# A two-attention, two-feed-forward kernel on one core: the second attention's first batch prepared inside the last chunk of the first feed-forward

## The reference, cut to what matters

```python
x = x + ffn0(attention0(x, mask, Wq, Wo), lut, gate_idx, up_idx, down_idx)
x = x + ffn1(attention1(x, cond, W_emb, b_emb, g_norm, W_qkv, g_q, g_k, W_out), Wr, br, Wg, Wu, Wd)
```

```python
xn = rms_norm(x1, g_norm) * (1 + scale) + shift      # one factor per row: rsqrt(mean(x1^2) + eps)
q, k, v = split(xn @ W_qkv)                          # 16 heads of 16
q, k = rms_norm(q, g_q), rms_norm(k, g_k)
o = softmax(q k^T / 4) v ;  result = o + o @ W_out
```

## Time and profile before

| | us |
|---|---|
| median of 3 runs (lowest, highest) | 706.95 (706.39, 708.73) |
| the profiled execution's own time | 707.92 |
| its span | 706.2 |
| PE busy | 580.7 (82%) |
| DVE busy | 419.2 (59%) |
| ACT busy | 326.3 (46%) |
| GpSimd busy | 118.9 (17%) |

### The profile page before, as it was taken

One profiled execution on the slowest core, in us unless ns is written; L12 is line 12 of the kernel. 1 busy time (PEld: TensorE's weight loads), 2 busy tenths in 40 slices (PEclk: granted clock), 3 DMA queues, 4 the chain that ended last, 5 costly groups with the idle time before them and its releaser, 6 DMA issues.

```text
span 706.2 us, 15569 instructions
## 1 busy us (share of the span) xinstructions
PE 580.7 (82%) x5115; PEld 347.5 (49%) x5147; DVE 419.2 (59%) x943; ACT 326.3 (46%) x592; POOL 118.9 (17%) x161
## 2 busy tenths in 40 slices
PE   3798989899976999995688777775199999999992
PEld 1344445455534655552354554443156666666661
DVE  1678698989853334343799999996523333333330
ACT  2456667677752332342677777773022222222220
POOL 4221122121511000000000000000203333322211
PEclk9999899999986999997799999997599999999996
DMA  8844345454851000005556666551101111011110
GB/s 295 202 95 113 90 110 123 113 121 108 156 134 32 1 1 0 0 0 125 159 120 150 149 147 148 132 137 46 24 22 46 45 45 41 31 37 37 45 32 3
DMA packets 29413, 60.27 MB, mean 85 GB/s; under 512 B 5989, under 2 KB 16647, under 8 KB 26952
## 3 DMA queue, kind: packets, MB, share of 16 engines
q1 hardware_dynamic: 20624, 25.68, 12.4%
q0 software_dynamic: 6432, 18.46, 12.2%
q10 hardware_dynamic: 2328, 15.75, 9.6%
HBM read 58.75 MB, written 7.81 MB: 94 GB/s over the span
## 4 chain that ended last, share of the span: by engine, by line
PE 27%; DVE 14%; issue 7%; ACT 3%; DVEq 1%; DMA 0%; POOL 0%; POOLq 0%; ACTq 0%
PE PA L1134 8%; PE PD L1153 7%; PE PB L1134 7%; PE PC L1142 2%; DVE arena L1479 2%; DVE small L1451 1%; ACT small L661 1%; DVE ms L1405 1%; DVE newt L1373 1%; PE PB L1020 1%; DVE rs L1379 1%; DVE newt L1376 1%; DVE small L1433 1%; DVE small L1437 1%; PE PD L1122 1%
## 5 line engine op out<-in xcount | busy, mean ns | idle before, releaser
L1231 DVE TENSOR_REDUCE nmax<-PB 128x2 f32<-128x512 f32 x128 | 85.5, 681 | 27.0 <-PE PB L808 25.4
L529 ACT ACTIVATE probs<-PC 128x512 f32<-128x512 f32 x128 | 73.9, 609 | 21.6 <-PE PC L820 20.6
L737 ACT CAST probs<-PC 128x1024 bf16<-128x1024 f32 x19 | 19.2, 1012 | 113.7 <-PE PC L1142 113.7
L1625 DVE TENSOR_TENSOR probs<-PC,probs 128x1024 bf16<-128x1024 f32 x19 | 23.3, 1225 | 80.9 <-ACT probs L737 80.9
L1134 PE MATMUL PA<-arena,probs 128*128 x227 | 53.7, 387 | 7.6 <-issue 3.8
L808 PE MATMUL PB<-small 64*128 64x256 bf16 x256 | 52.4, 297 | 8.2 <-DVE nmax L1231 6.1
L1153 PE MATMUL PD<-arena,probs 128*128 x456 | 54.5, 277 | 2.5 <-issue 2.5
L820 PE MATMUL PC<-small 64*128 64x256 bf16 x256 | 48.1, 289 | 3.8 <-DVE small L1247 3.5
L1153 PEld LDWEIGHTS PD<-arena,probs 128*128 128x128 bf16 x456 | 45.0, 99 | 9.0 <-issue 3.2
L1134 PE MATMUL PB<-arena,probs 128*128 x210 | 48.6, 379 | 0.9
L444 POOL DMA_DIRECT2D arena<-in_w_all x16 | 8.5, 532 | 236.7 <-DVE arena L1479 139.5
(11 more groups left out here) (201 smaller groups left out, 1163.9 us busy)
## 6 DMA issues: line engine op xcount, KB each, us to landing
arena<-idx_low ACTq DMA_DIRECT2D x15, 1024.0 KB
wst<-in_w_all SPq DMA_DIRECT2D x48, 256.0 KB, 2.7
arena<-in_w_all POOLq DMA_DIRECT2D x16, 384.0 KB, 5.9
arena<-in_idx_all SPq DMA_DIRECT2D x1, 2176.0 KB, 10.1
arena<-in_cond SPq DMA_DIRECT2D x16, 128.0 KB, 9.3
small<-in_x SPq DMA_DIRECT2D x16, 128.0 KB, 10.0
arena<-idx_low POOLq DMA_DIRECT2D x2, 1024.0 KB, 14.9
tok_r<-rows SPq DMA_DIRECT2D x1, 2048.0 KB, 14.4
```

What stands on the lines that cost most here:

```text
L529: nc.scalar.activation(probs[:, c, o], PC[:, o], ACT.Exp, scale=SCALE0).then_inc(S["ex"], 1)
L1231: v.tensor_reduce(nmax[:, c, s, :], PB[:, s * 512:(s + 1) * 512].rearrange("p (a k) -> p a k", k=T), AX.X, ALU.max, negate=True).then_inc( ...
L1625: v.tensor_tensor(hT_lo, PC[:], hT_hi, ALU.subtract).then_inc(S["hTl"], 1)
```

## The change

In the first attention, GpSimd's body(i) waits for `ct` of batch i-2 before it makes the product for batch i+2, and `max_columns` writes the absent column first, ahead of the last maximum. In the feed-forward all four chunks are written out; the down sums stand in PC alone, two to a bank, and DVE adds them with two instructions in place of four. PD is so free, and `turn_x(0)`, `queries_keys(0)`, `values1(0)`, `turn_x(1)` with ACT's and DVE's part of them stand between the pieces of chunk 3. The row factors are computed for batches 0 to 7 in chunk 2, and for batches 8 to 15 behind body1(0).

```diff
             def body(i, par, half, before=True, after=True):      # GpSimd
+                if before:
+                    pool.wait_ge(S["ct"], i - 1)
                 if after:
                     pool.wait_ge(S["pq"], 2 * i + 2)
                     projected(i + 2, par, half)
...
+            def totals(c):                                        # ACT
+                for t in range(TPC):
+                    sum_squares(TPC * c + t)
+            def earlier(c):
+                return lambda m: totals(c - 1) if m == MT // 2 - 1 else None
+            def meanwhile3(m):
+                if m == 0:
+                    act.wait_ge(S["gcol"], 6)
+                    act.wait_ge(S["rstd"], 2 + 3 * NEWTON)
+                    scaled(0)
+                if m == 1:
+                    modulated(0, PD)
+                if m == 2:
+                    squares(0, PD)
+                    scaled(1)
+                if m == 3:
+                    values1(0, 0, PD)
+                    totals(2)
+                if m == 4:
+                    modulated(1, PD)
+            gate_chunk(0, lambda m: None)
+            gate_chunk(1, earlier(1))
+            gate_chunk(2, earlier(2))
+            gate_chunk(3, meanwhile3)
...
             high_parts(0)
             body1(0, 0, before=False)
+            totals(3)
             body1(1, 1, before=False)
+            act.wait_ge(S["rstd"], 2 * (2 + 3 * NEWTON))
...
                     for t in range(TPC):                          # PE, down(m)
-                        o = (PC, PD)[t // 2][:, (t % 2) * 512:(t % 2) * 512 + T]
+                        o = PC[:, t * T:(t + 1) * T]
...
-                up(0)
-                if isinstance(c, int):
-                    outputs0(LAST)
-                    norm_and_router()
-                for m in range(1, MT):
+                for m in range(MT):
                     up(m)
-                    down(m - 1)
+                    if m > 0:
+                        down(m - 1)
+                    between(m)
                 down(MT - 1)
-            chunk(0)
-            with pe.Fori(1, TOK // CH) as c:
-                chunk(c)
...
+            def meanwhile3(m):                                    # PE
+                if m == 0:
+                    pe.wait_ge(S["c"], B)
+                    pe.wait_ge(S["w2"], 1)
+                    pe.wait_ge(S["wqkv"], 16)
+                    turn_x(0, PD)
+                if m == 1:
+                    queries_keys(0, PD)
+                if m == 2:
+                    values1(0, PD)
+                if m == 3:
+                    turn_x(1, PD)
...
-            turn_x(0)
-            queries_keys(0)
-            values1(0)
-            turn_x(1)
+            pe.wait_ge(S["hf"], MT * (TOK // CH))
+            pe.wait_ge(S["x1"], B)
             body1(0, 0, before=False)
...
             def max_columns(b):                                   # DVE
-                dve.wait_ge(S["max"], 8 * b + 8)
+                cols = mcol.rearrange("p q r (s m) -> p r s q m", s=2)
                 unless_first(dve, S["mt"], b)
+                v.tensor_copy(mcol[:, :, :, ROW_ABSENT::64].rearrange("p q r s -> p q (r s)"),
+                              nbig[:, :, bass.ds(b, 1)].broadcast_to([P, KT, 2 * PAIRS])).then_inc(S["mc"], 1)
+                maximum(b, 3, 1)
+                dve.wait_ge(S["max"], 8 * b + 8)
                 v.tensor_copy(cols[:, :, :, :, ROW_MAX], nmax[:]).then_inc(S["mc"], 1)
...
-                for t in range(TPC):                              # DVE, end of a chunk
+                for t in range(0, TPC, 2):
+                    o = slice(TPC * c + t, TPC * c + t + 2)
+                    v.tensor_tensor(rows[:, o, T:2 * T], PC[:, t * T:(t + 2) * T].rearrange("p (b t) -> p b t", b=2),
+                                    xall[:, o, :], ALU.add).then_inc(S["x1"], 2)
...
+            def row_scales(h, steps):                             # DVE: the 12 steps on batches 8h to 8h+7
+                o = slice(h * B // 2, (h + 1) * B // 2)
+                for k in steps:
+                    if k == 0:
+                        dve.wait_ge(S["ssq"], (h + 1) * B // 2)
...
+            def meanwhile2(m):                                    # DVE
+                if m == 4:
+                    row_scales(0, range(6))
+                if m == 5:
+                    row_scales(0, range(6, HALVES))
+            def meanwhile3(m):
+                if m == 3:
+                    mean_squares(0)
+                    for k in range(4):
+                        factors(0, k)
+                if m == 4:
+                    for k in range(4, STEPS):
+                        factors(0, k)
+                    scaled_qk(0)
+            hidden_chunk(0, lambda m: None)
+            hidden_chunk(1, lambda m: None)
+            hidden_chunk(2, meanwhile2)
+            hidden_chunk(3, meanwhile3)
             low_parts(0)
             body1(0, 0, 0, results=False, before=False)
+            row_scales(1, range(HALVES))
             body1(1, 1, 0, results=False)
```

More of the change, by code:

```diff
@@ L603, in sum_squares, with gate_chunk @@
                                      scale=T ** -0.5, accum_out=ssq[:, bass.ds(b, 1)]).then_inc(S["ssq"], 1)
-            def gate_chunk(c, before=True):
+            def gate_chunk(c, between):
                 for m in range(MT):
-                    if m == MT // 2 and before:
-                        for t in range(TPC):
-                            sum_squares(TPC * (c - 1) + t)
                     n = P if m < MT - 1 else MLAST
@@ L633, in scaled, with modulated @@
                                      ).then_inc(S["xr"], 1)
-            def modulated(b):
+            def modulated(b, bank=PB):
                 act.wait_ge(S["xt3"], b + 1)
@@ L957, in _, with chunk @@
             pe.wait_ge(S["w0"], LCH)
-            def chunk(c):
+            def chunk(c, between):
                 pe.wait_ge(S["ch"], TPC * c + TPC)
                 pe.wait_ge(S["cl"], TPC * c + TPC)
-                tok = bass.ds(c * CH, CH)
+                tok = slice(c * CH, (c + 1) * CH)
                 def up(m):
@@ L1292, in _ @@
             low(1)
-            for c in range(4):
-                for s in range(2):
-                    maximum(0, c, s)
+            for n in range(7):
+                maximum(0, n // 2, n % 2)
             max_columns(0)
@@ L1336, in _, with hidden_chunk @@
             dve.wait_ge(S["gcol"], 6)
-            def hidden_chunk(c):
+            def hidden_chunk(c, between):
                 for m in range(MT):
@@ L1342, in hidden_chunk @@
                     k = MT * c + m
-                    if isinstance(c, int) and m == 1:
+                    if k == 1:
                         dve.wait_ge(S["cl"], B)
@@ L1351, in hidden_chunk @@
                     v.tensor_tensor(h_lo[0:n, m, :], hf[0:n, m % 2, :], h_hi[0:n, m, :], ALU.subtract).then_inc(S["hl"], 1)
+                    between(m)
                 dve.wait_ge(S["dn"], MT * c + MT)
-                for t in range(TPC):
-                    b = TPC * c + t
-                    v.tensor_tensor(rows[:, bass.ds(b, 1), T:2 * T],
-                                    (PC, PD)[t // 2][:, (t % 2) * 512:(t % 2) * 512 + T].unsqueeze(1),
-                                    xall[:, bass.ds(b, 1), :], ALU.add).then_inc(S["x1"], 1)
-            hidden_chunk(0)
-            with dve.Fori(1, TOK // CH) as c:
-                hidden_chunk(c)
+                for t in range(0, TPC, 2):
+                    o = slice(TPC * c + t, TPC * c + t + 2)
+                    v.tensor_tensor(rows[:, o, T:2 * T], PC[:, t * T:(t + 2) * T].rearrange("p (b t) -> p b t", b=2),
+                                    xall[:, o, :], ALU.add).then_inc(S["x1"], 2)
             def guess(y, x):
@@ L1520, in body1 @@
                 weight_low(i, 2, par, half)
-            mean_squares(0)
-            for k in range(STEPS):
-                factors(0, k)
-            scaled_qk(0)
+            def meanwhile2(m):
[16 more added lines that the diff above has]
+            hidden_chunk(3, meanwhile3)
             low_parts(0)
             body1(0, 0, 0, results=False, before=False)
+            row_scales(1, range(HALVES))
             body1(1, 1, 0, results=False)
```

88 lines of the change are left out of this document (43 added, 45 removed).

## The result

The change makes the kernel faster by 0.64%: the ratio of its runs to those of the kernel before on the same chip is 0.9936 (95% interval 0.9907 to 0.9966), which is 4.5 us of 703 (2.4 to 6.5). The medians are 701.62 us after and 703.52 before, over 20 executions each. The ratio leaves out the executions in a slower state (four of the 20 of the changed kernel), the medians don't, and so they lie only 1.9 us apart. The forecast was no change that can be told, 1.45 us faster.

A forecast was written before the change was run, and what follows sets the result against it. Bounds: body length in the first attention, PE in the feed-forward, single steps then the weights' landing behind chunk 3. Terms -7.2 + 7.75 - 3.65 + 0.95 + 0.7 = -1.45 us, from 706.95 to 705.5; range 700 to 711.5.

The forecast's parts named there:

- The bound behind chunk 3: First weight_low waits for weights landing 14.5 us after issue, so 14.95 us behind the row sums; gain 3.65 us.
- Chunk 3: Inserted steps cost 3.6 us of PE work plus 4.75 of waits, less 0.6: row sums 7.75 us later.
- PE's waits in its first two pieces: In chunk 3, PE stands 2.15 us before turn_x(0) and 1.05 before queries_keys(0), behind ACT's rounding.
- The second half of the factors: Behind body1(0), ACT's late totals(3) and twelve DVE steps put weight_low(1, 0) at 11.6 us, costing 0.95.
- The product beside L1225: First attention: GpSimd's moved product costs nothing beside L1225, by the skill's rule; at most 5.9 us in all.
- The index rows' stream: Rival: the already late stream takes back the first attention's 7.2 us, giving 712.7 us; chance 0.16.
- The clock did not fall inside chunk 3: Rival: PE's pauses in chunk 3 halve its clock, 2.4 us more, 708 to 710 with slow body1(1); chance 0.17.
- The first attention's term: Later GpSimd product and earlier absent column save 0.65 us a body over eleven bodies: 7.2 us faster.
- The slow clock's term: After PE stands 8 us, body1(1)'s products run at clock 0.50: 0 to 1.5 us, taken as 0.7.
- The loop's joints: Feed-forward written out: PE pauses of up to 0.2 us at the loop's three joints go, saving 0.5 us.
- The pause at 64 us: Rival: PE's 2 us issue pause and the slow clock behind it vanish, 4.9 us, giving 700.6; chance 0.10.
- the start of the second attention is gained as meant: Rival: weights no bound, weight_low(0, 0) 4.3 us behind the row sums, 10.65 earlier, about 695 us; chance 0.07.

The follow-up runs named there:

- e5: Changed kernel with SP's first six weight pieces queued ahead of the 2 MB store of tok_r; 694.17 us, ratio 0.9864 to the kernel before.
- e3: Kernel before with only the new order in max_columns (absent column ahead of the last maximum); 703.86 us, ratio 0.9998.
- e2: Kernel before with only GpSimd's wait for ct; 696.58 us, ratio 0.9881.
- e11: Repeat of e1: kernel before with GpSimd's wait and the new order of the maxima; 694.04 us, ratio 0.9875.
- e1: Kernel before with GpSimd's wait for ct and DVE's new order of the maxima; 693.44 us, ratio 0.9833.
- e9: Control: e1 with SP's queue paced as in e6; 693.91 us, ratio 0.9867 to the kernel before.
- e8: Changed kernel with e6's pacing and the second half of the row factors ahead of the first weight_low; 692.50 us, ratio 0.9799 to the kernel before.
- e4: Changed kernel without GpSimd's wait and the new order: interleaved chunk 3 and factors in halves alone; 714.36 us, ratio 1.0167 to the kernel before.
- e10: e8 with each of the four inserted steps of chunk 3 one piece later on PE; 688.24 us, ratio 0.9805 to the kernel before.
- e6: Changed kernel, six weight pieces ahead of the tok_r store, SP waiting for wsh0 between three and three; 695.93 us, ratio 0.9894 to the kernel before.

## Why the prediction was wrong

**What held.** The bound behind chunk 3 was the landing of the weights, with 14.56 us behind the row sums where 14.95 was predicted, and e5 shows it by removal. Chunk 3 cost 7.55 us (7.75 predicted). PE's waits in its first two pieces were 1.99 and 0.89 (2.15 and 1.05). The second half of the factors cost 0.69 (0.95), but that agreement is in part luck: the 10.65 us of before, against which both are counted, passed at a mean granted clock of 0.68, and the prediction took them for the normal length; at 1.00 (e3) it is 9.05. GpSimd's wait was worth the subtraction's 0.54 and a little more, in every body (0.66 and 0.74 in turn, e2). The product beside L1225 (now L1250) cost nothing. The index rows' stream took nothing back: the two waits at the end of the stage are 12.2 us as before. The clock did not fall inside chunk 3.

**What failed is the sum, in several terms at once.** Beside each other, predicted and measured in the two profiles:

| term | predicted | measured |
|---|---|---|
| first attention, end of body 2 to end of body 14, without the pause | -7.2 | -8.2 |
| chunks 0 to 3 | +7.75 | +7.55 |
| first weight_low behind the row sums | -3.65 | -4.04 |
| second half of the factors | +0.95 | +0.69 |
| slow clock behind it | +0.7 | +1.6 |
| from the router's start to the end | 0 | -1.1 |
| sum | -1.45 | -3.5 |

*The first attention's term* was mis-sized: from the end of body 2 to that of body 14 it was 134.2 us before, if the long body is counted with 11.25, and is 126.0 now. The step that failed is "11.25 - 10.63 = 0.62 us", rounded up to 0.65 a body. Bodies take turns at two lengths, 11.21 and 11.29 before; 11.25 is their mean, and 10.63 is a body of the longer kind. Like beside like, the wait alone gives 0.74 and 0.66 (e2: 10.47 and 10.63), and wait and order together 0.76 and 0.77 (10.45 and 10.52). The eleven bodies sum to 8.07 us, not 7.2, and body 14, in which no product was in the way, adds 0.11. The timed executions say the same of this term: the first part alone gains 8.8 to 11.7 us (e11, e1). *The slow clock's term* was too small by 0.9: in the stretch from the second `weight_low` to the router two products run at 1.2 GHz, and it is 140.03 us for 138.44. The least certain row is the one above it, the second half of the factors: beside e2, e3 and e9, whose distance is 9.05 to 9.54 with the same steps as before, it would be 1.8 to 2.3. *The loop's joints* gave nothing: chunks 0 to 2 are as long as before (first silu to chunk 3's first silu 73.33 and 73.32), so the 0.5 us for them is wrong, and chunk 3's own work and waits were over-sized by 0.7. *The router and the experts* are 1.1 us shorter (211.98 for 213.05). No experiment speaks to the cause of this; the eight kernels with written-out chunks show 212.0 to 212.9 there, of the six with the loop five show 213.0 to 213.2 and e3 212.0.

The measured sum, -3.5, lies inside the interval of the ratio (-6.5 to -2.4); -1.45 lies outside it. But the table is not the whole difference of the two profiles, which is 11.0 us: 4.9 are the pause, 0.3 lie between body 14 and the first silu, and 2.4 lie ahead of the end of body 2 (48.18 for 50.59 us). Of the six other written-out kernels with the same first attention five reach that point at 50.2 to 50.5 us and one (e8) at 54.4, so I count the 2.4 to the single execution, which is a judgement and not shown. As far as the rows go, the steps that decided the verdict are thus the size of the gain in the first attention (1.0) and the stretch behind the router's start that was priced at nothing (1.1), against a bound of 0.3% (2.1 us) that the forecast's own sum came within 0.7 of.

**The pause at 64 us.** This rival came true in the profiled execution. The body that took 16.12 us before takes 10.52. The pause (1.8 to 2.7 us of PE at issue, in a body 15.3 to 16.5 us long) is in the profiled execution of all six kernels whose chunks are a loop (before, e1, e2, e3, e9, e11) and in none of the eight whose chunks are written out. "Nothing in the change touches that issue" was therefore a weak reason: something in the program's form goes with it. Its 4.9 us don't show in the timed ratios, though: the changed kernel is 4.5 us faster, not 8 to 9, and e4, which also lacks the pause, measures 11.7 us slower where its profiled span is 4.5 longer. The profiled execution of the kernel before, 707.92 us, less the pause would be 703.0, close to its median of 703.5; that would fit a pause that most timed executions don't have. But timed executions leave no such rows, so whether they have it stays open, and so does its cause.

**The unseen alternative.** The forecast took the landing of 14.5 us as a fixed figure. It was a consequence of the order on SP's queue: the pieces stood behind a 2 MB store that nothing waits for at that point. The rival "the start of the second attention is gained as meant" was rightly held unlikely for this change, and e5 makes it true by moving one line: `weight_low` 5.80 us behind the row sums where it named 4.3 (the product at the lower clock took 1.64 us longer, about the difference), and 158.2 us to the router.

## What to carry to other kernels

Work that was interleaved into a stage already bound by one engine cost its full time there plus a wait for each helper that had not finished its own piece; with each step one piece later than the earliest legal place, little more than its own time was left (e10: 3.68 us of 7.55, for some 3.6 us of products by the prediction's rows). Before steps are brought forward, look at what becomes late next, here a transfer queued behind a large store that nobody needs soon, and change the order of that queue with them. When a gain is a few tenths of a us in a repeated body, compare like with like: here the bodies alternate by 0.08 to 0.16 us, and the one body taken as the reference was of the longer kind.

## What the runs showed of the hardware

DVE's two-input subtraction of 16 columns takes 0.77 us when GpSimd's product of 256 columns starts just before it (e4, the kernel before) and 0.23 when it doesn't; reductions that read PSUM are not touched by the same product (1.95 us for three, with it or without). The Trainium skill (SBUF — State Buffer, "Who interferes with whom") says that a reduction never contends with GpSimd, and the trace agrees. For L1250, which reads one operand from PSUM and which the prediction priced at nothing by the same section, the trace agrees too as far as it goes: with 0.23 us beside the product it takes 0.39 us, and without it 0.38 to 0.39.

A 256 KB piece took 14.0 us to land when queued behind the 2 MB store, and three such pieces took a median of 5.2 us when queued ahead of it, with nothing but GpSimd's two high parts beside them (e6). PE's clock was 0.50 behind pauses of about 2 us in several places (68 to 74 us in the kernel before, after 1.96 us of nothing; 345 to 351 us in the changed kernel, after 2.13), but the changed kernel had 1.99 us of waiting inside chunk 3 with dense products around it and kept 1.00 there.
